# Four heads' new-value products joined into one of 512 columns, in the attention stage of a long one-core kernel

## The reference, cut to what matters

```
q, k, v = projections of x                    # 32 query heads, 8 kv heads, d = 128
k_all = concat([k_cache[block_table], k])     # 512 cached keys + the sequence's new ones
v_all = concat([v_cache[block_table], v])
scores = einsum('bqhd,bkhd->bhqk', q, k_all) / sqrt(128)
scores = where(valid, scores, -1e30)          # cached keys at or past cache_seqlens are masked
o = einsum('bhqk,bkhd->bqhd', softmax(scores), v_all)
```

## Time and profile before

| | |
|---|---|
| median of 3 runs | 3391.04 us (3390.39 to 3391.32) |
| profiled execution | 3392.49 us, span 3390.7 us |
| busy over the span | PE 97%, PEld 89%, DVE 67%, ACT 52%, POOL 39% |
| attention stage, line 2623 on PE | 4096 instructions, 542.0 us busy |
| attention stage, line 2482 on ACT | 512 copies, 142.2 us busy, 279.7 us idle before them, until PE |
| DMA over the span | mean 169 GB/s, 571.93 MB |

### The profile page before, as it was taken

One profiled execution on the slowest core, in us unless ns is written; L12 is line 12 of the kernel. 1 busy time (PEld: TensorE's weight loads), 2 busy tenths in 40 slices (PEclk: granted clock), 3 DMA queues, 4 the chain that ended last, 5 costly groups with the idle time before them and its releaser, 6 DMA issues. The chain is left out here.

```text
span 3390.7 us, 69362 instructions
## 1 busy us (share of the span) xinstructions
PE 3281.0 (97%) x22398; PEld 3026.4 (89%) x22398; DVE 2257.2 (67%) x6132; ACT 1763.5 (52%) x4307; POOL 1338.1 (39%) x2391
## 2 busy tenths in 40 slices
PE   7799999999899999999899999999999999999999
PEld 5688899987778888888899999999999998888878
DVE  6445644445478787788888888878888886323274
ACT  4323322233337788888666666666666665322222
POOL 0231100000017888888566666656666663100002
PEclk9899999999999999999999999999999999999999
DMA  5413422334645555556766666656666675533353
GB/s 207 136 58 71 127 82 80 86 105 144 208 143 184 173 170 175 185 175 207 244 219 221 213 221 220 220 186 216 217 221 219 213 231 189 173 106 102 114 184 103
DMA packets 448050, 571.93 MB, mean 169 GB/s; under 512 B 171657, under 2 KB 330185, under 8 KB 430794
## 3 DMA queue, kind: packets, MB, share of 16 engines
q1 hardware_dynamic: 427978, 429.08, 39.8%
q0 software_dynamic: 19712, 138.42, 11.6%
HBM read 394.60 MB, written 172.75 MB: 167 GB/s over the span
## 5 line engine op out<-in xcount | busy, mean ns | idle before, releaser
L2623 PE MATMUL l2a_x<-l2a_pt,l2a_V 128*128 128x128 f32 x4096 | 542.0, 275 | 0.8 <-DVE l2a_pn L2557 0.8
L2623 PEld LDWEIGHTS l2a_x<-l2a_pt,l2a_V 128*128 128x128 f32 x4096 | 498.6, 192 | 1.1 <-issue 1.1
L2535 DVE CUSTOM_DVE_ANT_0 l2a_sm<-l2a_s,l2a_B 128x544 f32<-128x544 f32 x512 | 370.2, 723 | 153.1 <-PE l2a_s L197 144.7
L2344 POOL CAST l2a_K<-cache 128x256 fp32r x768 | 306.9, 449 | 226.6 <-issue 226.6
L2489 ACT ACTIVATE l2a_p<-l2a_sm,l2a_st 128x544 f32<-128x544 f32 x512 | 379.8, 742 | 25.5 <-DVE l2a_st L2535 25.3
L2344 POOL CAST keys<-cache 128x256 fp32r x750 | 303.2, 451 | 175.2 <-issue 175.2
L2475 ACT ACTIVATE l2a_pt<-l2a_t 128x512 f32<-128x512 f32 x512 | 305.6, 597 | 102.1 <-PE l2a_t L2606 102.0
L2606 PE MATMUL l2a_t<-ident,l2a_p 128*128 128x128 f32 x2048 | 307.4, 273 | 5.2 <-ACT l2a_ao L2482 5.2
L2482 ACT ACTIVATE l2a_ao<-l2a_x 128x128 f32<-128x128 f32 x512 | 142.2, 278 | 279.7 <-PE l2a_x L2624 279.7
L2547 DVE TENSOR_SCALAR l2a_p<-l2a_p,l2a_st 128x512 f32<-128x512 f32 x512 | 270.7, 529 | 18.3
L197 PE MATMUL l2q_pa<-keys,cache 128*128 128x512 f32 (+1 forms) x1024 | 266.6, 342 | 3.4 <-DVE head L143 3.4
(11 more groups left out here) (855 smaller groups left out, 8592.3 us busy)
## 6 DMA issues: line engine op xcount, KB each, us to landing
s_qT<-l2q_qo SPq DMA_DIRECT2D x128, 512.0 KB, 2.8
head<-s_qT SPq DMA_DIRECT2D x64, 512.0 KB, 6.0
l2a_Q<-s_qT SPq DMA_DIRECT2D x64, 512.0 KB, 5.3
s_ao<-l2a_ao SPq DMA_DIRECT2D x64, 512.0 KB, 6.1
l2o_a<-s_ao SPq DMA_DIRECT2D x128, 256.0 KB, 3.0
s_kn<-l2q_ko SPq DMA_DIRECT2D x128, 128.0 KB, 2.9
head<-s_kn SPq DMA_DIRECT2D x32, 512.0 KB, 6.0
wqraw<-in_wqkv SPq DMA_DIRECT2D x32, 384.0 KB, 3.7
```

What stands on the lines that cost most here:

```text
L2344: e.tensor_copy(K[:, j:j + 1, :, :].rearrange("p a z n -> p a (z n)"), Kall[:, bass.ds(v, 1), :, :].rearrange("p a z n -> p a (z n)")).the ...
L2535: dve.tensor_tensor_reduce(out=smr[sc % 2][:, :], in0=ps_s[sc % 2][:, 224:768], in1=Br[g % 2][:, :], scale=-SCALE, scalar=3e38, op0=ALU.ad ...
L2623: pe.matmul(px[:, P:256], V[:, k * D + hg * P:k * D + hg * P + P], pt[:, k, :], start=k == 0, stop=False)
```

## The change

The four heads' products with the new values become one. The new values of the four heads are loaded as one 128x128 tile (head h in partitions 32h to 32h+31, no zeros), split into high and low parts by ScalarE and GpSimd (`VN`, "vnew"). The turned pnew is split too (`nT`, "pnT": high by ScalarE, low by VectorE), and four transfers from ScalarE's own queue lay its 32-row bands on the diagonal of `dg` ("diag", 128 x 2 x 512, zero elsewhere). Three products of 512 columns then add the new part to all four heads at once, behind the last head's cached-value products. The four heads' outputs lie side by side in one bank, which ScalarE copies out once a group. pnew is turned one step later, in the step of the group's first value products. VectorE's new keys move to hg = 2 and its mask to hg = 3.

```diff
@@ buffers
-    Nr = st.slots("vn", 2, [P, 4, P], each=4)
+    Nr = st.slots("vn", 2, [P, P], each=4)
+    VN = [st.pair(f"vnew{i}", [P, P]) for i in range(2)]
+    nT = st.sb("pnT", [P, 2, P], F32R)
+    dg = st.slots("diag", 1, [P, 2, D], F32R, each=4)
@@ SyncE
                 if g >= 2:
-                    sp.wait_ge(pv_mm, 4 * (g - 1))
+                    sp.wait_ge(values_lo, g - 1)
                 for h in range(4):
-                    sp.dma_start(Nr[g][32 * h:32 * h + 32, h, :],
+                    sp.dma_start(Nr[g][32 * h:32 * h + 32, :],
...
-                    sp.wait_ge(o_copied, pv + 1)
+                    sp.wait_ge(o_copied, pv // 4 + 1)
@@ GpSimd
-            for z in Nr.bufs:
-                pool.memset(z[:, :, :], 0.0).then_inc(cleared, 1)
+            pool.memset(dg[0][:, :, :].bitcast(F32), 0.0).then_inc(cleared, 1)
...
+            def low_values(g):
+                pool.wait_ge(values_hi, g + 1)
+                low_part(pool, [z[:, :] for z in VN[g % 2]], Nr[g][:, :]).then_inc(values_lo, 1)
...
                 if hg == 1 and g:
                     values(g)
+                if hg == 2 and g:
+                    low_values(g - 1)
@@ ScalarE
-                    act.wait_ge(pv_mm, pv + 1)
-                    if pv % 8 == 0 and k >= 2:
-                        act.wait_ge(*ao.landed(k - 2))
-                    act.activation(ao[k][:, hg, :, 32 * (g % 2):32 * (g % 2) + 32],
-                                   ps_x[pv % 2][:, P:256].rearrange("p (h s) -> p h s", h=4), ACT.Copy).then_inc(o_copied, 1)
+                    if hg == 0:
+                        act.wait_ge(new_turned, g + 1)
+                        if g:
+                            act.wait_ge(*dg.landed(g - 1))
+                        act.activation(nT[:, 0, :], ps_x[(g + 1) % 2][:, 0:P], ACT.Copy).then_inc(new_hi, 1)
+                    if hg == 1:
+                        act.wait_ge(new_lo, g + 1)
+                        if g:
+                            act.wait_ge(new_mm, g)
...
+                        for h in range(4):
+                            at = slice(32 * h, 32 * h + 32)
+                            act.dma_start(dg[g][at, :, P * h:P * h + P].bitcast(F32), nT[at, :, :].bitcast(F32)).then_inc(dg.sem(g), 16)
+                    if hg == 3:
+                        act.wait_ge(new_mm, g + 1)
...
+                        act.activation(ao[k][:, :, :, 32 * (g % 2):32 * (g % 2) + 32].rearrange("p g h s -> p (g h) s"),
+                                       ps_x[g % 2][:, :].rearrange("p (h s) -> p h s", s=32), ACT.Copy).then_inc(o_copied, 1)
+                if i % 4 == 0 and 4 <= i <= U:
+                    g = i // 4 - 1
+                    act.wait_ge(*Nr.landed(g))
+                    if g >= 2:
+                        act.wait_ge(new_mm, g - 1)
+                    act.activation(VN[g % 2][0][:, :], Nr[g][:, :], ACT.Copy).then_inc(values_hi, 1)
@@ VectorE
-                if tr is not None and tr % 4 == 0:
...
-                    dve.tensor_copy(pnr[g % 2][:, :], ps_x[tr % 2][:, 0:P]).then_inc(new_copied, 1)
+                if pv is not None and pv % 4 == 0:
+                    g = pv // 4
+                    dve.wait_ge(new_hi, g + 1)
+                    dve.tensor_tensor(nT[:, 1, :], ps_x[(g + 1) % 2][:, 0:P], nT[:, 0, :].bitcast(F32), ALU.subtract).then_inc(new_lo, 1)
@@ TensorE
-                        pe.wait_ge(o_copied, tr - 1)
...
+                        pe.wait_ge(newed, pv + 4)
+                        if g:
+                            pe.wait_ge(o_copied, g)
+                        pe.transpose(ps_x[(g + 1) % 2][:, 0:P], pNr[g % 3][:, :], ident[:, :]).then_inc(new_turned, 1)
...
-                        pe.matmul(px[:, P:256], V[:, k * D + hg * P:k * D + hg * P + P], pt[:, k, :], start=k == 0, stop=False)
-                    pe.matmul(px[:, P:256], vn[:, hg, :], pnr[g % 2][:, :], start=False, stop=True).then_inc(pv_mm, 1)
+                        m = pe.matmul(px[:, P * hg:P * hg + P], V[:, k * D + hg * P:k * D + hg * P + P], pt[:, k, :],
+                                      start=hg + k == 0, stop=False)
+                    m.then_inc(pv_mm, 1)
+                    if hg == 3:
+                        pe.wait_ge(*dg.landed(g))
+                        pe.wait_ge(values_lo, g + 1)
+                        mm3(pe, px[:, :], [([z[:, :] for z in VN[g % 2]], (dg[g][:, 0, :], dg[g][:, 1, :]))], start=False).then_inc(new_mm, 1)
```

More of the change, by code:

```diff
@@ L2306, in l2_attn @@
     ptr = [st.sb(f"pt{i}", [P, 4, P]) for i in range(2)]
-    pnr = [st.sb(f"pn{i}", [P, P]) for i in range(2)]
     str_ = [st.sb(f"st{i}", [P, 8]) for i in range(4)]
@@ L2312, in l2_attn @@
     inverted, scaled, newed = (st.sem(n) for n in ("inverted", "scaled", "newed"))
-    turned, new_turned, t_copied, new_copied, pv_mm, o_copied = (
-        st.sem(n) for n in ("turned", "new_turned", "t_copied", "new_copied", "pv_mm", "o_copied"))
+    turned, new_turned, t_copied, new_hi, new_lo, pv_mm, new_mm, o_copied, values_hi, values_lo = (
+        st.sem(n) for n in ("turned", "new_turned", "t_copied", "new_hi", "new_lo", "pv_mm", "new_mm", "o_copied", "values_hi", "values_lo"))
     change = {4 * (NB - 2) + 2: 4, 4 * (NB - 2) + 3: 5, 4 * (NB - 1): 6, 4 * (NB - 1) + 2: 7}
@@ L2455, in _ @@
                     page_copies(pool, r, n, range(10, 16), pages_g)
+            low_values(G - 1)
         @block.scalar
@@ L2478, in _ @@
                     k = pv // 8
-                    act.wait_ge(pv_mm, pv + 1)
-                    if pv % 8 == 0 and k >= 2:
-                        act.wait_ge(*ao.landed(k - 2))
-                    act.activation(ao[k][:, hg, :, 32 * (g % 2):32 * (g % 2) + 32],
-                                   ps_x[pv % 2][:, P:256].rearrange("p (h s) -> p h s", h=4), ACT.Copy).then_inc(o_copied, 1)
+                    if hg == 0:
[7 more added lines that the diff above has]
+                            act.wait_ge(new_mm, g)
+                        else:
+                            act.wait_ge(cleared, 1)
+                        for h in range(4):
[3 more added lines that the diff above has]
+                        act.wait_ge(new_mm, g + 1)
+                        if g % 2 == 0 and k >= 2:
+                            act.wait_ge(*ao.landed(k - 2))
+                        act.activation(ao[k][:, :, :, 32 * (g % 2):32 * (g % 2) + 32].rearrange("p g h s -> p (g h) s"),
[6 more added lines that the diff above has]
+                    act.activation(VN[g % 2][0][:, :], Nr[g][:, :], ACT.Copy).then_inc(values_hi, 1)
                 if sc is not None:
@@ L2512, in mask @@
                 half, b = divmod(g, NB)
-                if g:
-                    new_keys(g)
                 if g >= 2:
@@ L2564, in _ @@
                         if hg == 2:
+                            new_keys(n)
+                        if hg == 3:
                             mask(n)
@@ L2584, in _ @@
                         if sc > LV:
-                            pe.wait_ge(o_copied, sc - LV)
+                            pe.wait_ge(new_lo, (sc - LV) // 4 + 1)
                         keep_busy(pe, ps_x[1][:, 0:P], ident[:, :], fill[sc])
```

21 lines of the change are left out of this document (6 added, 15 removed).

## The result

The changed kernel takes **3557.8 us** (median of 4 runs, 3552.7 to 3563.2) where the kernel before takes 3391.2 in the same comparison: a ratio of 1.049, 95% interval 1.047 to 1.051. The forecast was 3405 us with a range up to 3450. The sign was right; the loss is 167 us where 14 were expected. One of the two executions of a kernel further down (rows first, no transfers) ran at a granted clock of 0.76 over the whole and took 4026.9 us, and is left out. Where a kernel's time stands without a ratio, it is that of one execution.

The account below looks back on a forecast made before the run. TensorE, 100.00 of 100 us busy in the attention stage, was taken as the bound. 3392.5 - 27.1 (tensor products) + 40 (late value rows) + 1 (stage's end) = 3406.4, less 1.5 gives 3405 us; full range 3362 to 3450.

Parts of the forecast that it names:

- The tensor products: Attention stage, TensorE: 1024 old instructions removed (114.2 us), 384 products of 512 columns added (87.1 us), net -27.1 us.
- Rival 3: TensorE's joined products cost 0.05 us more each than in a long run: +19 us, 3383 without a stall; counted within spread.
- the chain behind the rows: ScalarE's work from the value rows' landing until TensorE may turn pnew: wait, copies, exponential and read, landing + 2.07 us.
- rival 2: Diagonal or its issue late in every group, 0.5 us each: 3428 us, 3445 with half the value-row stall; chance 0.22.
- the first stall: TensorE's stall from late value rows: 0.2 to 1.1 us, middle 0.65, in 62 groups, +40 us.
- The value rows: New V rows, fetched behind the output store in every second group, reach ScalarE late, at +8.3 to +9.2: +40 us.
- joint: The end of a group's last product on TensorE, the zero from which the forecast counts its + times in us.
- ScalarE's issues: Four transfer issues a group on ScalarE, 0.42 us each, covered by its idle time of about 3.0 us: priced zero.
- the cover: ScalarE's slack before TensorE needs pt; gone at 2.2 us for the four issues, beyond which every microsecond stalls TensorE.
- The diagonal: Last transfer lands in 2 to 3.3 us, before the joined product: zero; ends 1.5 (zero) and 4.6 us (166 us).
- rival 4: VectorE becomes the bound; 8.0 of 9.2 us busy spoke against it; chance 0.03.
- the waits at the stage's end: End of attention stage: output-copy waits go, last diagonal has no scores to hide behind, 1 to 2 us each; net +1.

Follow-up runs that it names:

- the kernel with neither loss: Changed kernel without the four transfers and their landing waits, SyncE fetching value rows before the output store; 3364.3 us in its profiled execution.
- the direct form: Changed kernel without transfers, ScalarE and VectorE writing the four 32-partition bands straight onto the diagonal, all computed; 3510.2 us, ratio 1.034.

## Why the prediction was wrong

**The tensor products: right.** -27.1 us was forecast, and the kernel with neither loss shows 3364.3, groups of 9.19. Rival 3 (0.05 us dearer each) falls with it. (Slips of the working that change nothing: 1024 x 0.112 is 114.7 and not 114.2, the chain behind the rows adds up to 2.03 and not 2.07, and rival 2 with half of the first stall is 3448 and not 3445.)

**The value rows: the mechanism right, the landing wrong.** This is the step that failed first: "If the rows come earlier by all of that, they land at +8.3; if by none, at +9.2". Without transfers they were at ScalarE at joint + 0.82 + 9.40 = +10.2 on average. By the forecast's own rule (each microsecond after +8.1 is one of the tensor engine) that is 2.1 us in 62 groups, 131 us in place of 40; measured, rows first against store first, 163. The granted clock over the whole is 0.977 in one and 0.987 in the other, which may be the rest (below); no run separates it. The miss has two parts. The landing was taken from one group, 8.6 us behind the store; counted over 25 such groups of the kernel before it is 9.0 (8.2 to 9.8), over all 63 it is 8.8. And the gather's earlier start was to bring the rows up to 0.9 us earlier, and brought nothing: taking it back moved them from 9.40 to 9.13. The sign of that small effect is open, since in the direct form, with the gather 1.0 us ahead of the store, they arrive at 8.75. The spread between 8.3 and 9.2 left no room for "later", though the row loads' longest landing, 7.5 us against the median of 4.7, stood in the earlier trace rows.

**ScalarE's issues: mis-sized.** 0.42 each was taken from SyncE's row loads, another shape of transfer; it is 0.62, four of them 2.8 us on average, above the 2.2 at which the forecast said the cover is gone. Priced at zero; they cost 98 us with the rows in time, 0.77 a group.

**The diagonal: the condition was named, the wrong side taken.** "I take a landing in 2 to 3.3 us, so zero." From the fourth issue's start, from which the forecast counted, it lands after 3.5 us on average in the changed kernel and 4.2 in the one with the rows first. And that issue starts at +5.8 to +6.0 and not at +5.2, which leaves 2.6 us and not 3.3. The landing taken, 2 to 3.3, holds for the few groups with nothing beside the transfers (1.9). For the others, the forecast held the tail of the gather against them and left out the q load, which its rival 2 named; it goes out beside them in 81 of the 128 groups. The end stated, 4.6 us and 166 us in all, was almost the price, 162 measured, by luck: a shorter landing and a later issue made up for each other. Rival 2 is therefore what happened in part, with both of its conditions met, but its price of 0.5 us a group was a quarter of the 2.0 (260 us over 128 groups) that transfers cost with the rows in time.

The rule that was weighed for this in the prediction, that each DMA engine goes round its queue rows packet by packet (the Trainium skill, "DMA: Bandwidth & Descriptors", section "Queues, rings and completion order"), was to take rival 2 away. It did not. Going round packet by packet still leaves an engine to share with every other row that has work, and the traces show that sharing: 1.25 us after the issues with nothing of SyncE's beside the transfers, 2.83 with q and rows, 4.35 with the keys as well. The rule was no reason for a joined product that does not wait.

**How they add.** Alone, the rows cost 163 us and the transfers 260 over 3364; together they would make 3787, and the kernel takes 3558. (The 260 was measured with the row loads going out beside the transfers, as the new order of SyncE has it, so it is too high for the changed kernel.) A stall in one place gives time to the other wait: the diagonal is waited for in 64 groups and not in 102, the rows in 43 and not in 62. That is why removing the transfers wins 31 us and moving the rows' copy none. The rows-first complete kernel is 67 us slower than the changed one because its row loads now go out beside the transfers in every group: the landing over all groups is 3.5 us, 2.9 in the changed kernel and 3.1 with the row loads left out, which gives back 46 of the 67. The rest is open.

**The rest held.** VectorE did not become the bound of the changed kernel (rival 4; 77.55 of 100), and the waits at the stage's end are too small to be seen.

## What to carry to other kernels

Where a change puts a transfer or a queue position into a loop that runs at 100% of one engine, price the issue and the landing at the slow end of all such rows in the profile, not at one of them, and count how often each microsecond comes back: here 128 times. Ask what the other queues send at the same moment. And count a landing over all groups: a count over those that waited hides the quick ones, and made two experiments here look as if nothing beside the transfers mattered. When two waits hide each other, removing one shows almost nothing; take both away once, to see what the arithmetic is worth, and then put them back singly. A saving of 0.21 us a group paid for none of the data movement that made it possible.

## What the runs showed of the hardware

An SBUF-to-SBUF transfer of 32 partitions, two pieces of 512 B each, took 0.59 us of the issuing queue at the least, on ScalarE and on SyncE, and ScalarE's next work stood behind it; SyncE's row loads, one such piece each, take 0.42. The last of four landed 1.25 us after its issue had ended where nothing of SyncE's went out beside them, 2.83 beside a q load of 512 KB and row loads, and 4.35 beside two loads of 512 KB and row loads.

Reading and writing 32 partitions of 128 columns is hardly cheaper than all 128. In the direct form, ScalarE's bands and VectorE's (instructions of one line, busy us and mean ns):

```profile
L2493 ACT ACTIVATE l2a_diag<-l2a_x 32x128 fp32r<-32x128 f32 x509 | 134.3, 264 | 9.4
...
L2579 DVE TENSOR_TENSOR l2a_diag<-l2a_x,l2a_diag 32x128 fp32r<-32x128 f32 x512 | 146.9, 287 | 28.9 <-ACT l2a_diag L2493 22.7
```

ScalarE takes 0.26 us for a quarter of the partitions, where the copy of all 128 took 0.28; VectorE takes 0.287, and 0.285 for the subtraction on all 128 in the changed kernel.

The clock fell behind a long wait. After 2.20 us of idle in the kernel without transfers the tensor engine worked for 1 us as before; then 3.5 us were granted 0.57 of the clock, near its 1.2 GHz level, and eight V products took 1.92 us in place of 1.06:

```profile
2442.93 0.30 PE L2635 MATMUL l2a_x<-ident,l2a_pnew 128*128 128x128 f32 x1 [2.20 <-ACT l2a_ao L2498]
2443.06 1.12 PE L2643 MATMUL l2a_x<-l2a_pt,l2a_V 128*128 128x128 f32 x8
...
2445.93 1.92 PE L2643 MATMUL l2a_x<-l2a_pt,l2a_V 128*128 128x128 f32 x8
```

```profile
2443.90:2447.40 3.50, 3.50 (x20) 3.50 (x19) 3.11 (x11) 2.22 (x7) 1.10 (x3) 0.57 0.58 212
```
